# Row halves for the 192-row projections, a prologue that mixes them with the maxima, and the scan's inputs on VectorE

## What is computed

```python
q = (query @ Wq + bq).reshape(B, Nq, H, D).transpose(0, 2, 1, 3)
k = (key_value @ Wk + bk).reshape(B, Nkv, H, D).transpose(0, 2, 1, 3)
v = (key_value @ Wv + bv).reshape(B, Nkv, H, D).transpose(0, 2, 1, 3)
attn = jnp.einsum('bhqd,bhkd->bhqk', q, k) * scale
attn = jnp.clip(attn, -CLAMP, CLAMP)
attn = jax.nn.softmax(attn, axis=-1)
x = jnp.einsum('bhqk,bhkd->bqhd', attn, v).reshape(B, Nq, Cq)
return x @ Wo + bo
```

```python
deltaA = jnp.exp(delta[..., None] * A)
deltaB_u = delta[..., None] * Bm[:, :, None, :] * xi[..., None]
def step(state, inputs):
    dA_t, dBu_t, C_t = inputs
    state = dA_t * state + dBu_t
    y_t = jnp.einsum('bdn,bn->bd', state, C_t)
    return (state, y_t)
y = ys.transpose(1, 0, 2) + xi * D
y = y * _silu(res)
```

## Time and profile before

| | us |
|---|---|
| median of 3 runs | 1336.77 |
| lowest, highest | 1335.69, 1338.14 |
| the profiled execution, its own time | 1334.81 |
| its span in the trace | 1332.7 |
| TensorE busy in the span | 1192.7 (89%) |
| VectorE, ScalarE busy | 714.2, 715.0 (54% each) |
| GpSimd busy | 224.8 (17%) |

### The profile page before, as it was taken

One profiled execution on the slowest core, in us unless ns is written; L12 is line 12 of the kernel. 1 busy time (PEld: TensorE's weight loads), 2 busy tenths in 40 slices (PEclk: granted clock), 3 DMA queues, 4 the chain that ended last, 5 costly groups with the idle time before them and its releaser, 6 DMA issues.

```text
span 1332.7 us, 29487 instructions
## 1 busy us (share of the span) xinstructions
PE 1192.7 (89%) x12749; PEld 768.2 (58%) x12749; DVE 714.2 (54%) x1351; ACT 715.0 (54%) x995; POOL 224.8 (17%) x118
## 2 busy tenths in 40 slices
PE   8999999999999999316699899999999999999566
PEld 6356666666666666206598356666555666666344
DVE  2565555555555663668223546555555555575332
ACT  3356666666666667242213356666666666667322
POOL 0222122222222200033000222222222211110000
PEclk9699999999999999557799799999999999999668
DMA  8444444444433360610803744444433334360540
GB/s 187 115 105 105 105 105 105 105 101 88 101 89 88 68 171 2 217 63 0 314 2 90 174 104 105 105 102 88 98 83 90 86 86 104 84 160 3 205 135 5
DMA packets 80947, 138.18 MB, mean 104 GB/s; under 512 B 9064, under 2 KB 72176, under 8 KB 80304
## 3 DMA queue, kind: packets, MB, share of 16 engines
q1 hardware_dynamic: 79920, 136.16, 41.2%
q10 hardware_dynamic: 896, 0.12, 0.1%
HBM read 57.96 MB, written 0.15 MB: 44 GB/s over the span
## 4 chain that ended last, share of the span: by engine, by line
PE 76%; DVE 17%; ACT 2%; DMA 2%; issue 2%; POOL 0%; SPq 0%; ACTq 0%; DVEq 0%; POOLq 0%
PE ring L543 41%; PE st L543 17%; PE ot L543 15%; DVE mpart L1221 9%; DVE arena L1348 2%; DMA qst<-rowb 2%; PE ring L674 1%; DVE arena L1352 1%; ACT arena L932 1%; PE ring L549 0%; PE ring L642 0%; DVE work L1342 0%; DMA warena<-ctxT 0%; POOL arena L532 0%; DVE work L1296 0%
## 5 line engine op out<-in xcount | busy, mean ns | idle before, releaser
L1221 DVE TENSOR_REDUCE mpart<-ring 128x1 f32<-128x448 f32 x896 | 515.8, 618 | 402.2 <-PE ring L543 400.0
L955 ACT ACTIVATE work<-st 128x1024 f32<-128x1024 f32 x392 | 401.2, 1023 | 169.5 <-PE st L543 165.2
L543 PE MATMUL ring<-arena,qst 96*128 96x448 bf16 x896 | 298.6, 367 | 4.3 <-DVE mpart L1221 2.5
L543 PE MATMUL ot<-work,arena 128*17 128x128 f32 x6272 | 247.5, 275 | 2.1 <-ACT work L955 1.1
L543 PE MATMUL st<-qst,arena 97*128 97x128 bf16 x3136 | 241.1, 219 | 5.8 <-DMA qst<-rowb 5.4
L543 PEld LDWEIGHTS st<-qst,arena 97*128 97x128 bf16 x3136 | 196.1, 98 | 67.7 <-issue 29.2
L543 PEld LDWEIGHTS ot<-work,arena 128*17 128x17 f32 x6272 | 137.6, 96 | 142.1 <-issue 94.3
L495 POOL TENSOR_TENSOR arena<-arena 128x896 f32<-128x896 f32 x52 | 98.2, 1888 | 692.1 <-ACT arena L928 692.0
L543 PE MATMUL ring<-warena,wkv 96*128 96x448 f32 x448 | 192.1, 558 | 1.5 <-DVE mpart L1221 1.3
L543 PE MATMUL ring<-wkv,warena 96*128 96x256 f32 x784 | 188.4, 383 | 1.0 <-DVE mpart L1221 1.0
L543 PEld LDWEIGHTS ring<-wkv,warena 96*128 96x128 f32 x784 | 146.2, 190 | 28.2 <-DVE mpart L1221 11.3
(11 more groups left out here) (278 smaller groups left out, 640.3 us busy)
## 6 DMA issues: line engine op xcount, KB each, us to landing
arena<-arena SPq DMA_DIRECT2D x336, 224.0 KB, 5.1
warena<-ctxT SPq DMA_DIRECT2D x28, 672.0 KB, 5.0
arena<-ffn_W SPq DMA_DIRECT2D x16, 1024.0 KB, 12.4
arena<-f SPq DMA_DIRECT2D x2, 4096.0 KB, 24.3
arena<-scratch_bc SPq DMA_DIRECT2D x1, 2048.0 KB, 6.9
arena<-rows SPq DMA_DIRECT2D x1, 1792.0 KB, 6.8
warena<-w_in_proj SPq DMA_DIRECT2D x1, 1024.0 KB
warena<-w_W SPq DMA_DIRECT2D x1, 1024.0 KB, 6.9
```

The lines of the kernel that those rows point to most:

```text
L543: return nc.tensor.matmul(o, l, r, start=start, stop=stop, **kw)
L955: nc.scalar.activation(pbuf[:, n % 2], st[:, 2 * (n % 2):2 * (n % 2) + 2].rearrange("p b k -> p (b k)"), ACT.Exp).then_inc(*signal(f"{lay} ...
L1221: V.reduce_max(mpart[:, 2 * h + hf:2 * h + hf + 1], ring[:, BANKS[step][0], 0:HALF], AX_X).then_inc(*signal(f"{lay}_b_max"))
```

## The change

Five things change.

1. **Row halves.** The contraction over 192 rows is cut as 128 + 64 rows. The 64-row tails of the context and of the weights are loaded twice, into partitions 0 to 63 and 64 to 127. `k` and `v` steps come in pairs: the first step of a pair issues only its 128-row products, the second issues its own and then the tails of both, for one bank from the lower row half and for the other bank from the upper one. `k_full` and `v_full` rise by 2 at the end of the pair. For a context load SyncE issues three DMAs in place of one, 256 rows of 896 in place of 192.
2. **The plan.** The prologue mixes keys 1, values 1 and half of keys 2 with the maxima of chunk 0. In the loop a pair stands in one unit (values in units 0 and 2, keys in 5 and 7).
3. **Even maxima.** From chunk 1 on `per_unit` goes from (1, 1, 1, 1, 3, 2, 2, 2, 2, 3, 4, 3, 4, 3) to (1, 3, 1, 3, 3, 1, 3, 1, 3, 3, 2, 3, 2, 3).
4. **Identity products.** `keep_clock` calls of 2 to 30 products are put in front of waits in all blocks but the cross-attentions.
5. **Scan block on VectorE.** `dBu` is made by VectorE in place of GpSimd; the gate `sres` moves behind the making of `xi`, its reciprocal in two halves.

```diff
+    def pair(kind, c, first):
+        return [(kind, c, first), (kind, c, first + 1)]
+
+    plan = pair("k", 0, 0) + [("k1", 0, 0)] + pair("k", 0, 2) + [("k2", 0, 0), ("k1", 0, 1), ("k2", 0, 1)]
+    plan += pair("v", 0, 0) + pair("v", 0, 2) + pair("k", 1, 0) + some(6, 0)
+    plan += pair("k", 1, 2) + [("k1", 1, 0)] + some(6, 0) + [("k1", 1, 1)]
+    plan += pair("v", 1, 0) + some(3, 0) + [("k2", 1, 0)] + some(3, 0)
+    plan += pair("v", 1, 2) + some(3, 0) + [("k2", 1, 1)] + some(4, 0)
+    plan += pair("k", 2, 0) + some(7, 0)
+    plan += [("row", 0, 0)] + pair("k", 2, 2) + score(0) + score(1)
...
+    values = {0: (0, 1), 2: (2, 3)}
+    keys = {5: (0, 1), 7: (2, 3)}
     firsts, seconds = {7: 0, 9: 1}, {10: 0, 11: 1}
     for c in range(NCH):
-        per_unit = ((4,) * 8 + (0,) if c == 0 else (1, 1, 1, 1, 3, 2, 2, 2, 2)) + (3, 4, 3, 4, 3)
+        per_unit = ((4,) * 8 + (0,) if c == 0 else (1, 3, 1, 3, 3, 1, 3, 1, 3)) + (3, 2, 3, 2, 3)
         for u in range(UNITS):
             if c + 2 < NCH and u in values:
-                plan.append(("v", c + 2, values[u]))
+                plan += [("v", c + 2, n) for n in values[u]]
             if c + 3 < NCH and u in keys:
-                plan.append(("k", c + 3, keys[u]))
+                plan += [("k", c + 3, n) for n in keys[u]]
...
+        TAILS = (slice(0, TAIL), slice(TAIL, P))
...
             def load_ctx(lay, par, at):
-                load(ctxt[0:CP, par], a["ctxT"].rearrange("(k p) n -> p k n", p=CP)[:, :, bass.ds(at, CK)],
-                     f"{lay}_ctx_in{par}")
+                load(ctxt[:, par, 0], a["ctxT"][0:P, at:at + CK], f"{lay}_ctx_in{par}")
+                for part in range(2):
+                    load(ctxt[part * TAIL:(part + 1) * TAIL, par, 1], a["ctxT"][P:CC, at:at + CK],
+                         f"{lay}_ctx_in{par}")
 
...
-            pool.wait_ge(*done_of("dtu_ready"))
-            pool.wait_ge(sem("bc_in"), 16)
-            for b in range(NB):
-                if b >= 2:
-                    pool.wait_ge(sem("scanned"), b - 1)
-                nc.gpsimd.tensor_tensor(
-                    m_["dBu"][:, b % 2].rearrange("p (n t) -> p n t", n=NS),
-                    m3["dtu"][:, b:b + 1].broadcast_to([P, NS, TOK]),
-                    m_["bc"][:, 0:NS * TOK].rearrange("p (n t) -> p n t", n=NS), ALU.mult).then_inc(*signal("dBu_ready"))
...
-            def keep_clock(n):
+            def keep_clock(n, bank=4):
 
                 for _ in range(n):
-                    mm(pb[4][:, 0:P], ident, ident)
+                    mm(pb[bank][:, 0:P], ident, ident)
...
                         m, hf = n // 2, n % 2
                         if n == 0:
-                            pe.wait_ge(sem(f"{lay}_ctx_in{c % 2}"), 16 * (c // 2 + 1))
-                        project(ring[:, bank, 0:HALF], lambda k: wkv[:, k, 0, m * P:(m + 1) * P],
-                                lambda k: ctxt[0:CP, c % 2, k, hf * HALF:(hf + 1) * HALF], f"{lay}_k_full", 2)
+                            pe.wait_ge(sem(f"{lay}_ctx_in{c % 2}"), 16 * PROJECTION_LOADS * (c // 2 + 1))
+                        mm(ring[:, bank, 0:HALF], wkv[:, 0, 0, m * P:(m + 1) * P],
+                           ctxt[:, c % 2, 0, hf * HALF:(hf + 1) * HALF], stop=False, skip_group_check=True)
+                        if hf:
+                            for half, rows_of in enumerate(TAILS):
+                                last = mm(ring[:, BANKS[(kind, c, n - 1 + half)][0], 0:HALF],
+                                          wkv[rows_of, 1, 0, m * P:(m + 1) * P],
+                                          ctxt[rows_of, c % 2, 1, half * HALF:(half + 1) * HALF], start=False,
+                                          skip_group_check=True)
+                            last.then_inc(sem(f"{lay}_k_full"), 2)
                     if kind == "v":
                         for t in range(2 * n, min(2 * n + 2, TPC)):
-                            last = project(ring[:, bank, (t % 2) * D:(t % 2 + 1) * D],
-                                           lambda k: ctxt[0:CP, c % 2, k, t * P:(t + 1) * P],
-                                           lambda k: wkv[:, k, 1, :], None, 2)
-                        last.then_inc(*signal(f"{lay}_v_full"))
+                            mm(ring[:, bank, (t % 2) * D:(t % 2 + 1) * D], ctxt[:, c % 2, 0, t * P:(t + 1) * P],
+                               wkv[:, 0, 1], start=(t % 2 == 0), stop=False, skip_group_check=True)
+                        if n % 2:
+                            for t in (2 * n - 2, 2 * n, 2 * n - 1, 2 * n + 1):
+                                if t < TPC:
+                                    rows_of = TAILS[t // 2 % 2]
+                                    last = mm(ring[:, BANKS[(kind, c, t // 2)][0], (t % 2) * D:(t % 2 + 1) * D],
+                                              ctxt[rows_of, c % 2, 1, t * P:(t + 1) * P], wkv[rows_of, 1, 1],
+                                              start=False, skip_group_check=True)
+                            last.then_inc(sem(f"{lay}_v_full"), 2)
...
             def mamba():
+                keep_clock(11, 6)
                 transpose2(tmp[0], 5, "rms_normed", "rmsT_full")
...
+                keep_clock(30, 6)
                 pe.wait_ge(*done_of("xi_ready"))
...
+                    if b == NB - 1:
+                        keep_clock(14, 6)
                     pe.wait_ge(sem("weighted"), b + 1)
...
             def linear_attention():
+                keep_clock(8)
                 transpose2(xn, 5, "G_normed", "GxT_full")
                 pe.wait_ge(sem("w1_in"), 16 * 8)
                 pe.wait_ge(*done_of("GxT_ready"))
                 for n, w in enumerate(("Wq", "Wk", "Wv")):
                     project(pb[n][:, 0:D], lambda k: xT[:, k], lambda k: w1[w][:, k], "Gqkv_full")
+                keep_clock(18)
                 pe.wait_ge(*done_of("Gqkv_ready"))
                 mm(pb[3][:, 0:D], l_["mean"], l_["qkv"][:, 0]).then_inc(*signal("Gqg_full"))
...
-                dve.wait_ge(*done_of("res_exp"))
-                sigmoid_of_exp(m2["sres"])
-                link(V.tensor_tensor(m2["sres"].rearrange("p b t -> p (b t)"), pb[1][:, :],
-                                     m2["sres"].rearrange("p b t -> p (b t)"), ALU.mult))
                 dve.wait_ge(*done_of("xc_exp"))
...
+                dve.wait_ge(*done_of("res_exp"))
+                link(V.tensor_scalar(m2["sres"], m2["sres"], 1.0, None, ALU.add))
+                V.reciprocal(m2["sres"][:, 0:NB // 2], m2["sres"][:, 0:NB // 2])
...
+                link(V.reciprocal(m2["sres"][:, NB // 2:], m2["sres"][:, NB // 2:]))
...
+                def inputs(b):
+                    V.tensor_tensor(m_["dBu"][:, b % 2].rearrange("p (n t) -> p n t", n=NS),
+                                    m3["dtu"][:, b:b + 1].broadcast_to([P, NS, TOK]),
+                                    m_["bc"][:, 0:NS * TOK].rearrange("p (n t) -> p n t", n=NS), ALU.mult
+                                    ).then_inc(sem("dBu_ready"), 1)
...
+                dve.wait_ge(sem("bc_in"), 16)
+                inputs(0)
+                link(V.tensor_tensor(m2["sres"].rearrange("p b t -> p (b t)"), pb[1][:, :],
+                                     m2["sres"].rearrange("p b t -> p (b t)"), ALU.mult))
                 for b in range(NB):
                     dve.wait_ge(sem("dA_ready"), b + 1)
                     dve.wait_ge(sem("dBu_ready"), b + 1)
...
+                    if b + 1 < NB:
+                        inputs(b + 1)
```

63 lines of the change are left out of this document (40 added, 23 removed).

## The result

| | before | after |
|---|---|---|
| median, us | 1337.45 (4 runs, 1335.69 to 1341.30) | 1357.87 (4 runs, 1355.21 to 1361.88) |
| span of the profiled execution | 1332.7 | 1355.2 |
| first layer's loop, first to last `pv` | 464.6 | 486.9 |
| second layer's loop | 465.4 | 491.0 |
| all the rest | 402.7 | 377.3 |

The change makes the kernel slower: ratio 1.0147, 95% interval 1.0124 to 1.0171. One execution of the kernel with the old numbers of maxima, further down, took 2345 us at a mean granted clock of 0.50 and is left out of that kernel's ratio; its median, 1285.05 with it, is 1284.30 without. The table tells where to look: outside the two loops 25 us are gained, in them 48 are lost.

What follows compares the result with a forecast made beforehand. TensorE was taken to bound the two loops (928 of 1333 us), VectorE's chain the scan stage. Gains of 28.6 + 26.4 + 6 + 4 + 12 + 4 + 8 = 89 us gave 1248 us, range 1230 to 1285.

Steps and rivals of the forecast that it cites:

- row halves, keys: Key pairs in both loops: each falls from 3.00 to 2.35 us; over 44 pairs a gain of 28.6 us.
- row halves, values: Value instructions, 12 chunks in each of 2 layers: 6.05 to 4.95 us a chunk, a gain of 26.4 us.
- waits in the loop: TensorE's waits in both loops: 0.3 us a chunk gained over 22 chunks, 6 us, between 0 and 0.75 a chunk.
- prologues: Both layers ahead of the first pv, the second layer's context wait included: 4 us gained, between -12 and +12.
- scan stage: VectorE's chain in the scan: shorter gate, faster input projection, inputs made by VectorE; 12 us gained, range 8 to 13.
- gates and experts: The 64 expert instructions, 9.64 us before: small products ahead lift the clock, gaining 4 to 5 us, 4 taken.
- behind the second layer: Linear attention and the sets: identity products cover part of each wait and lift the clock; 8 us gained (0 to 13).
- who is late next: Loop, units 7 to 11: even maxima remove about 1.5 us of waits, ScalarE's row becomes late; 0.3 us a chunk gained.
- rival (c): Row-half pairs: each tail drains the array before its neighbour starts; 190 us lost, 1438 us; chance 0.03.
- Full overlap: Key tails of a pair run side by side in the two row halves: 0.75 us, against 1.50 without overlap.
- The walk: Prologue followed step by step: maxima end at 54 us, first scores stand at 57.5, first pv 6.6 us earlier.
- the clock set against it: Prologue: a low clock makes each of five pairs 2.3 us longer, 11.5 in all; 4 us loss taken per layer.

Runs made afterwards that it cites:

- the run with the row first: Changed kernel with the row of unit 10 (copy, DMA, alpha) moved ahead of the cast k2 on ScalarE: 1277.50 us, ratio 0.9518.

## Why the prediction was wrong

By its own terms, in the profiled executions (a gain is positive):

| term | forecast | measured | from |
|---|---|---|---|
| row halves, keys | 28.6 | 20 | units with a pair, changed kernel |
| row halves, values | 26.4 | 21 | the same |
| waits in the loop | 6 | -89 | loops: -48 in all, less 41 |
| prologues | 4 | -1.5 | 0.3 and 1.2 later to the first `pv` |
| scan stage | 12 | 12.4 | last `pv` to the fourth block, 108.3 to 95.9 |
| gates and experts | 4 | 4.9 | 26.8 to 21.9 |
| behind the second layer | 8 | 9.6 | 92.8 to 83.2 |
| sum | 89 | -22.5 | 1332.7 to 1355.2 |

**The step that failed** is the one on who is late next: "The even maxima remove that part, and the row's way through ScalarE becomes late instead. I take 0.3 a chunk ... between 0 and 0.75". The 0.3 is what was to be left of the 1.5 us a chunk, a gain; the row's lateness inside it was priced at about 1.2 (a chunk of "about 33" against 31.8, "row waits near 1 us in unit 12"), and the clock at nothing. By the run with the row first the lateness costs 3.65 in each of 22 chunks, which is 80 of the 83 us between the two kernels' loops: about 49 in wait and 34 in clock. So the place was right, the wait was sized too low, and a cost was missing. Three things led to it. First, the slack wasn't read. The 0.3 came from averages over a chunk; the lines of the kernel before around 317.72 and 319.41 show that the row landed just as it was needed, and the edit of `per_unit` takes 0.46 us of TensorE's work out from between. Second, the DMA's duration was taken as fixed. Its place against SyncE's burst was 0.33 us; the same edit moves the burst ahead, since SyncE waits for TensorE's last scores. The prediction never asked what the earlier end of a chunk triggers. Third, the clock in the loop was taken as given, because it was 1.00 in every row; that a wait of 2 us could bring it down wasn't weighed, though the same rows show 0.64 for the scan stage with its idle TensorE. As rival (c) shows, I looked for the slower side in the array and not in a wait, and gave it 0.03.

"The even maxima remove that part" was wrong too. With two maxima unit 10 takes 2.60 us, 1.1 more than a unit with two maxima and no wait (1.49), so the waits there are still about 1 us. One long subtraction on GpSimd now meets the minimum of `m`: 0.82 us at the median, where it was 0.17 in every chunk of the kernel before. With the row on time the loops gain 35 us (930.0 - 894.9), less than the 41 of the row halves: the waits other than the row's are 6 us more than before, where 6 less was forecast.

**Row halves: mechanism right, size too large.** Full overlap: right, 0.745 us a key pair (3.40 - 2.65). But a pair holds 2.65, not 2.35. In the single records the first 128-row product after the maxima takes 0.480 us instead of 0.375, the way into the tails costs 0.093, and the first tail again 0.105 more; I had charged 0.10 for all of this. The values: 5.44 us a chunk with the pairs' slow starts, where before it was 6.30 with one (I had 4.95 from 6.05). Expected 55 in the loops, measured 41. (The key products alone, 3.00 to 2.65 in 44 pairs, make 15 of the 20 in the table; the rest is the units around them.)

**Prologue**: forecast 4, within -12 and +12; measured -1.5, which is less than kernels with this same prologue differ by. The walk was wrong and not the clock set against it: the last maximum of the first layer begins at 57.5 us and the first scores stand at 63.3 (62.44 before, 57.5 forecast), though the clock was at 0.50 for only 10 us of this prologue against 20 before. Between its groups of maxima TensorE waits 0.4 to 0.5 us for ScalarE's copies and 0.17 us for single maxima; which of them the walk left out stays open. In the second layer the 1.2 us are the wait for the larger context load (1.3 forecast); from the first key product to the first `pv` it is 53.5 us in both kernels.

**Scan stage, experts, linear attention**: right, and by the reasons given. The scans of the kernel after are all at 4.43 us, with inputs of 2.29 between them (chain of waits; 4.51 and 8.65 in the earlier trace rows):

```profile
604.40 4.44 DVE arena L1401
608.86 2.29 DVE arena L1405
...
613.49 4.44 DVE arena L1401
...
661.10 7.25 PE st L547 x64
```

The 64 expert instructions take 7.25 (9.64 in the earlier trace rows; forecast 6.9). Without the identity products the kernel is 20 us slower, of which I had expected 15.

The range failed for the same reason as the value. Its ends came from the row halves and the prologue, which came out 14 and 5.5 us below their values and inside their bounds. The waits had 0 to 0.75 us a chunk, all of it gain, with no row behind these two ends, and that term decided the sign. Small slips in the prediction's sums change none of this: its items for a chunk of TensorE add up to 34.35 and not 34.2, 22 x 0.3 is 6.6, and 14 value tails at 0.38 cost 3.6 a chunk and not 3.8, which puts rival (c) near 1433.

## What to carry to other kernels

When an edit takes work out of a stretch of the engine that bounds the kernel, list every wait at the end of that stretch and read its slack from the timeline (when the thing landed, when it was needed), before averaging anything; a slack of zero looks like no wait at all. A small DMA on the critical path must be issued ahead of the burst that the same point of the program releases: move its producer up, or make the burst wait. Spend a wait you can't avoid on identity products, since the low clock behind it cost here about 0.7 us for each us of the row's lateness (34 to 49).
